# Unread 512-column products ahead of each slot's scores in the first attention

## The reference, cut to what matters

```python
x = x + _L0_xattn_ref(_layernorm(x), ctx, ctx, Wq, bq, Wk, bk, Wv, bv, Wo, bo)
x = x + _L0_ffn_ref(_layernorm(x), ...)
x = x + _L1_xattn_ref(_layernorm(x), ctx, ctx, mask, mask, mask, Wq, Wk, Wv, Wo)
x = x + _L1_ffn_ref(_layernorm(x), ...)
```

```python
qh = (q @ Wq.T + bq).reshape(B, S, 16, 8).transpose(0, 2, 1, 3)   # kh, vh alike
scores = einsum('bhqd,bhkd->bhqk', qh, kh) / sqrt(8)
out = einsum('bhqk,bhkd->bhqd', softmax(scores), vh)
return out.transpose(0, 2, 1, 3).reshape(B, S, 128) @ Wo.T + bo
```

## Time and profile before

| | |
|---|---|
| median of 3 runs | 1699.14 us (1695.71 to 1699.17) |
| the profiled execution's own time | 1695.49 us |
| its span in the profile | 1693.7 us |
| mean granted clock of TensorE | 0.864 |
| TensorE busy | 1401.0 us, 83% of the span |
| VectorE, ScalarE, GpSimd busy | 949.1, 814.0, 661.4 us |
| first attention | about 40 to 345 us |

### The profile page before, as it was taken

How to read it: one execution, slowest core, us unless ns; L and a number is a source line. 1 busy time by engine, 2 the same in 40 slices (tenths; PEclk the granted TensorE clock), 3 DMA queues, 4 the chain that set the end, 5 groups by cost and what they waited for, 6 DMA issues and landing times. The chain is left out here.

```text
span 1693.7 us, 31779 instructions
## 1 busy us (share of the span) xinstructions
PE 1401.0 (83%) x11720; PEld 1123.0 (66%) x11720; DVE 949.1 (56%) x2066; ACT 814.0 (48%) x1335; POOL 661.4 (39%) x556
## 2 busy tenths in 40 slices
PE   0599999806599999999993798988988989836698
PEld 0477777606488888888882477777777777736486
DVE  0455544337656665666563666665666666527665
ACT  0255655521344444444442465655656556521354
POOL 1266656602155555555552123333232332412254
PEclk9999655555799999999996899998999899965799
DMA  4211111040000000000001000000000000010000
GB/s 114 75 39 39 46 63 45 2 149 1 1 1 1 1 1 1 0 0 0 0 0 62 1 2 1 2 1 3 2 1 3 2 1 2 2 32 1 1 25 25
DMA packets 27575, 31.59 MB, mean 19 GB/s; under 512 B 4721, under 2 KB 21682, under 8 KB 27314
## 3 DMA queue, kind: packets, MB, share of 16 engines
q1 hardware_dynamic: 27442, 29.75, 5.7%
HBM read 23.45 MB, written 6.29 MB: 18 GB/s over the span
## 5 line engine op out<-in xcount | busy, mean ns | idle before, releaser
L1347 POOL TENSOR_TENSOR w_lo_f<-weighted_f,w_hi_f 128x512 fp32r<-128x512 f32 x232 | 300.6, 1296 | 345.8 <-ACT w_hi_f L1289 345.8
L565 POOL TENSOR_TENSOR p_lo_l<-probs_l,p_hi_l 128x512 f16<-128x512 f32 x128 | 148.2, 1158 | 336.5 <-ACT p_hi_l L358 336.5
L1327 DVE TENSOR_TENSOR hidden_f<-psum,gate_act_f 128x512 f32<-128x512 f32 x232 | 160.5, 692 | 210.0 <-PE psum L1239 199.3
L1304 ACT ACTIVATE gate_act_f<-psum 128x512 f32<-128x512 f32 x232 | 138.7, 598 | 269.0 <-PE psum L1239 267.6
L916 POOL TENSOR_TENSOR p_lo_a<-probs_a,p_hi_a 128x1024 f16<-128x1024 f32 x64 | 135.9, 2127 | 112.9 <-ACT p_hi_a L808 112.9
L1333 DVE TENSOR_TENSOR weighted_f<-psum,hidden_f 128x512 f32<-128x512 f32 x232 | 160.5, 692 | 9.0
L1239 PE MATMUL psum<-x_lo_f,w_hi 128*128 (+1 forms) x384 | 153.8, 401 | 0.0
L1237 PE MATMUL psum<-x_hi_f,w_hi 128*128 (+1 forms) x384 | 152.0, 396 | 1.8 <-PEq L1135 1.8
L1238 PE MATMUL psum<-x_hi_f,w_lo 128*128 (+1 forms) x384 | 151.8, 395 | 0.0
L1289 ACT ACTIVATE w_hi_f<-weighted_f 128x512 fp32r<-128x512 f32 x232 | 144.9, 625 | 2.2 <-DVE weighted_f L1333 2.2
L356 ACT ACTIVATE probs_l<-psum,lift_l 128x512 f32<-128x512 f32 x128 | 88.0, 688 | 105.0 <-PE psum L232 105.0
(11 more groups left out here) (257 smaller groups left out, 3797.9 us busy)
## 6 DMA issues: line engine op xcount, KB each, us to landing
q_x_a<-spill SPq DMA_DIRECT2D x32, 128.0 KB, 2.6
k_x_a<-spill SPq DMA_DIRECT2D x32, 128.0 KB, 2.5
spill<-q_hl_a SPq DMA_DIRECT2D x8, 256.0 KB, 2.0
spill<-k_hl_a SPq DMA_DIRECT2D x8, 256.0 KB, 2.9
out<-x_all SPq DMA_DIRECT2D x8, 256.0 KB, 2.3
pick_raw<-c_pick SPq DMA_DIRECT2D x1, 1536.0 KB, 6.2
stage<-L_ffn_w SPq DMA_DIRECT2D x3, 256.0 KB, 3.0
stage<-L_xattn_Wq SPq DMA_DIRECT2D x1, 512.0 KB, 3.5
```

Of the source, the lines that this page charges most:

```text
L565: nc.gpsimd.tensor_tensor(p_lo[:, r, :], probs[:, r, :], p_hi[:, r, :], ALU.subtract).then_inc(s_exp_lo, 1)
L1304: nc.scalar.activation(gate_act[:, slot, :], GATE[slot][:, :], ACT.Silu).then_inc(s_silu, 1)
L1327: nc.vector.tensor_tensor(hidden[:, slot, :], UP[slot][:, :], gate_act[:, slot, :], ALU.mult).then_inc(s_hid, 1)
L1347: nc.gpsimd.tensor_tensor(w_lo[:, slot, :], weighted[:, (parity * nc_ + k) % 2, :], w_hi[:, slot, :].bitcast(F32), ALU.subtract).then_inc( ...
```

## The change

Before the score products of a slot, behind the two waits, a loop issues products of full height (128 rows) and 512 columns of fp16: the keys' high and low parts of the slot's sequence against the keys of the whole group, both from `k_x`. They write the first of the slot's two score banks, which the score products overwrite afterwards (they start with `start=True`). Nothing reads what they wrote. Slot 0 has 24 of them, each other slot three.

```diff
 RING0 = 4
+START_FULL, SLOT_FULL = 24, 3
...
                 if s >= 2:
                     pe.wait_ge(s_exp_hi, s - 1)
+                for _ in range(START_FULL if s == 0 else SLOT_FULL):
+                    nc.tensor.matmul(T_BANK[:, 2 * (s % 2), :], k_x[:, par, 0, tok], k_x[:, par, 0, :], start=True, stop=True)
                 for r in range(4):
```

## The result

The changed kernel takes 1756.8 us (median of 4 runs, 1744.3 to 1770.1) against 1697.4 us before; the ratio is 1.035 with a 95% interval of 1.027 to 1.043. It is slower, by 59 us where 30 were forecast: the sign held, the forecast was half of what came. Its profiled execution took 1752.2 us, span 1750.4, 56.7 us more than the span before. The runs spread over 26 us, those of before over 4.

A forecast was written before the change was run, and what follows sets the result against it. TensorE, mostly at 1.2 GHz, was taken to bound the first attention. Periods +15, last pairs +7 and slot 0 +7.3 made about +30 us on 1695.5, giving 1725.5, stated as 1726; range 1685 to 1758.

The forecast's parts named there:

- The price of a product: First attention, on TensorE's path: 0.43 us per product at 1.2 GHz, 0.23 at 2.4; 1.28 or 0.68 us per slot.
- the rival without grants: First attention: clock hardly held at 2.4 GHz beyond slot 0; +88 us, 1784, or 1765 with a few grants; chance 0.11.
- The forecast's own terms: Eight slots at 1.2 GHz: 45.3 us less waits filled by products, 0.5 after q, 0.3 each after v and x fills.
- Slot 0: Its 24 products cost 7.3 us, an estimate between 10.2 at 1.2 GHz and 5.5 at 2.4 GHz.
- The pair at 2.4 GHz: Two slots without fills, with products, at 2.4 GHz: 6.7 us, 0.5 less than in the kernel before.
- The share of work at 2.4 GHz: First attention: 0.55 in the six eight-slot periods, giving +15 us, and 0.5 in the last seven pairs, giving +7.
- My own two lines: With share f at 2.4 GHz: a period takes 44.3 - 13.9 f us; the last seven pairs add 17.9 - 21.4 f.
- The reason that I gave for losing the clock: Projection's end through wait, values, products, scores, values: only 0.68 us wide streaming in some 3.2; falls at even slots without fills.
- 0.7 us in a period: At 2.4 GHz, k and c fills give back 0.7 us per eight slots, waiting for ScalarE's copy of the maxima.
- The second half of the reason: The clock returns where q or x fill, transposition and next three products stand back to back, denser than an earlier grant's place.
- That the clock holds throughout: Rival for the first attention: 2.4 GHz nearly throughout, -19 us, 1676 us; chance 0.22.
- break-even: Share of the first attention's work at 2.4 GHz where gain and cost cancel, f = 0.82; above it the kernel is faster.

The follow-up runs named there:

- the kernel with narrow products: The changed kernel with its 213 products on 32 of the 128 rows, all else equal; 1785.6 us, ratio 1.052.
- the kernel with the same number elsewhere: The changed kernel with the even slot's three products moved from ahead of the scores to behind the projection; 1706.2 us, ratio 1.0045.
- seven per pair in the right places: Against the change: one product ahead of scores (three in slots 1 modulo 8), three behind even projections, two before odd attention transpositions, 12 at start; 1675.0 us, fastest.
- five per pair: As seven per pair in the right places, but no product ahead of the scores except in slots 1 modulo 8; 1699.3 us, ratio 1.000.

## Why the prediction was right or wrong

**The price of a product**: right. Low pairs measured 9.76 us (9.75 forecast); the kernel with narrow products, whose clock stayed low throughout, took 1785.6 us where the rival without grants was put at 1784. Its period without a grant took 45.0 us (slots 9 to 17), 44.3 forecast: the waits before the transposition of the maxima hid less of the products than I took off for them. (The forecast's own terms, 45.3 - 0.5 - 0.3 - 0.3, give 44.2.)

**Slot 0**: near, and in part by luck. The 24 products were put at 7.3 us and made slot 0's exponential 6.3 us late (79.36 against 73.09 us). Slot 1's own three products stand in no term of the sum, since the periods begin behind slot 1; with them it is 7.4. The burst alone, in the kernel without the others, cost about 4.

**The pair at 2.4 GHz**: 0.36 us short. I kept the wait for VectorE's addition at 0.48 us. In the changed kernel, in the high stretch and at 1.2 GHz:

```profile
220.79 1.23 DVE L859 TENSOR_REDUCE negmax_a<-psum 128x8 f32<-128x1024 f32 x1 [1.08 <-PE psum L688]
221.00 0.39 PE L724 MATMUL psum<-bo,ones 128*128 128x128 f32 x2
...
221.93 0.28 DVE L876 TENSOR_TENSOR x_all<-psum,x_all 128x128 f32<-128x128 f32 x1
...
347.56 1.23 DVE L859 TENSOR_REDUCE negmax_a<-psum 128x8 f32<-128x1024 f32 x1 [2.58 <-PE psum L688]
348.71 0.29 DVE L876 TENSOR_TENSOR x_all<-psum,x_all 128x128 f32<-128x128 f32 x1
```

At 2.4 GHz the projection is over at 221.39, but the addition starts only at 221.93: ahead of it in VectorE's stream stands the reduction of the maxima, which takes 1.23 us at either clock. At 1.2 GHz the reduction was over about when the projection was (348.67 us), and the addition followed at 348.71. This error is worth some 1 us in the changed kernel, which was seldom in that state; a whole period at 2.4 GHz took 31.2 us where I had 30.4.

**The share of work at 2.4 GHz**: this is the step that failed. I took 0.55 in the six periods and 0.5 in the last seven pairs. My own two lines, solved for what was measured, give 0.32 (44.3 - 13.9 f = 239.0 / 6) and 0.14 (17.9 - 21.4 f = 14.9). The sum had 15 + 7 where 33.8 + 14.9 came, and that is the missing 27 us. Of these 4 to 5 belong to the prices: with periods of 45.0 and 31.2 us my 0.55 would have given 19 instead of 15. The other 22 or so belong to the share. The clock itself says the same: 0.55 of the work is 46% of the time by my prices, an estimate, and the trace has 32%.

The reason that I gave for losing the clock, the stretch behind the projection, was right, but I gave it to the even slots without a fill alone. Three of the eleven falls came there. Eight came with a k fill or behind a c fill, before which TensorE stands idle for ScalarE's copy of the maxima. I had seen this wait and entered it only as a price, 0.7 us in a period; for the clock I counted these slots as safe, since the k fill had brought the grants of the kernel before. Products behind the projection in every even slot (the kernel with the same number elsewhere) took away the falls at k and c fills and won 51 us. Only then did the next place show, the v fill and the scores behind it without products; in the changed kernel itself no fall came there.

The second half of the reason held only in part. I expected the clock to come back at the q or x fills with the next three products. It did so at all four q fills that it met at 1.2 GHz, but at three of five x fills: those of slots 13 and 21 brought nothing, and around them lie the two stretches of 40 us. In the last 14 slots, where there is no fill at all, a clock once lost (329.9 us) didn't come back, which I had weighed at only one half. That each kind of place counts by itself is read from the traces; no run mended the k and c fills alone.

**The rivals.** That the clock holds throughout fell: the trace has 38.72 of 40 us busy at 0.50. The Trainium skill's advice to keep TensorE busy ("TensorE: Matmul & The Clock Gate", "Why this matters for your kernels") would have given 2.4 GHz there, and this trace disagrees. That the clock is hardly held (1765 to 1784) is nearer than break-even, and is exact for the narrow products. The range, 1685 to 1758, just held the median, but not two of the four runs (1761 and 1770).

## What to carry to other kernels

Work that is added to hold the clock pays only if it holds it: look in the trace for the places where it falls, and fill those first. Here they lay where TensorE waited for another engine, also right before dense work. Idle time of TensorE is where such work is cheap, and the same number of products cost 51 us less there than ahead of the critical scores. Too few can be worse than none and worse than twice as many: three per slot lost 59 us, six 40, seven per pair in the right places gained 24, and five per pair gained nothing.

## What the runs showed of the hardware

- The height of the products matters, not the time that they occupy: 213 products on 32 rows brought no grant at all in the stage, on 128 rows eleven. Heights between were not run.
- A share of busy time does not tell the clock: 97% busy at 1.2 GHz and 85% at 2.4 GHz in one trace.
- The profile's clock column shows full speed until the first recorded change. Durations or spacings of one form of product (628 ns, or 0.43 us apart, at 1.2 GHz) tell the truth.
- A kernel whose clock comes and goes spreads: over 4 runs each, 26 us for the change and 20 for five per slot, but 4 for the kernel before and for the fastest one, and 3 for the one without a grant.

Open: which rule the gate follows was not measured, only where in this kernel it gave and took. That two of seven like places in the kernel before brought a grant is put down to timing, which is argued and not shown. The record adds this: of the 38 executions of the kernel before that ran beside the experiments, 19 show a mean granted clock of 0.94 over the whole run, as the kernel without any grant in the stage does (0.942), and 19 show 0.84 to 0.89. So it seems that half of them had no grant in the stage at all; their traces were not kept.
